# Finishing stages of a graph attention network: pairs written out in groups three ahead, own row scaled on ACT, no arithmetic on POOL, elu by a maximum

## The reference, cut to what matters

```
h = elu(layer_norm(x @ w_in + b_in, g_in, bt_in))
for i in range(3):
    identity = h
    hp = (h @ w_l[i]).reshape(N, 4, 64)
    s = sum(hp * a_s, -1); d = sum(hp * a_d, -1)
    e = leaky_relu(s[src] + d[dst], 0.2)
    alpha = softmax of e over the edges that enter a node, its own loop among them
    y = segment_sum(hp[src] * alpha[:, :, None], dst) + b_l[i]
    y = layer_norm(elu(y), g_l[i], bt_l[i])
    h = y + identity
```

## Time and profile before

| | us |
|---|---|
| median of 3 runs | 7346.19 (7344.77 to 7347.49) |
| profiled execution | 7350.6 |
| its span | 7348.8 |
| busy: PE, DVE, ACT, POOL | 5337.8, 4937.3, 4115.6, 3961.0 |
| input stage, first transfer to the next stage's first | 135.43 to 340.66 |
| finishing stage 0 | 1488.11 to 1720.37 |
| finishing stage 1 | 2883.43 to 3116.30 |
| finishing stage 2 (no projection) | 4275.47 to 4459.39 |

### The profile page before, as it was taken

How to read it: one execution, slowest core, us unless ns; L and a number is a source line. 1 busy time by engine, 2 the same in 40 slices (tenths; PEclk the granted TensorE clock), 3 DMA queues, 4 the chain that set the end, 5 groups by cost and what they waited for, 6 DMA issues and landing times. The chain is left out here.

```text
span 7348.8 us, 96874 instructions
## 1 busy us (share of the span) xinstructions
PE 5337.8 (73%) x22394; PEld 3800.7 (52%) x22394; DVE 4937.3 (67%) x13271; ACT 4115.6 (56%) x13250; POOL 3961.0 (54%) x3916
## 2 busy tenths in 40 slices
PE   1768888644888886468887614999978778777578
PEld 1645555333555554445555314888864566555335
DVE  5656666685777777667777576666652677877673
ACT  4578888844898987468989742333336222111132
POOL 3477777656777774677777730000000577777322
PEclk8878888866999998679999767999999898878789
DMA  6344444335444443354444422000017534333302
GB/s 177 116 126 118 117 118 117 89 111 145 118 119 120 119 121 86 118 143 121 119 120 118 109 88 71 23 17 26 17 54 260 164 114 127 105 105 98 93 14 78
DMA packets 492147, 774.74 MB, mean 105 GB/s; under 512 B 86183, under 2 KB 367735, under 8 KB 491703
## 3 DMA queue, kind: packets, MB, share of 16 engines
q0 software_dynamic: 168240, 452.12, 22.8%
q1 hardware_dynamic: 323607, 319.65, 13.9%
HBM read 634.42 MB, written 146.27 MB: 106 GB/s over the span
## 5 line engine op out<-in xcount | busy, mean ns | idle before, releaser
L1699 POOL DMA_INDIRECT gm_got<-scratch_feat,keep_src_tab x2520 | 2535.7, 1006 | 785.3 <-issue 680.0
L1910 ACT ACTIVATE gm_got<-gm_got 128x64 f32<-128x64 f32 x10080 | 2453.6, 335 | 4.7 <-DVE gm_got L1833 4.7
L1958 PE MATMUL gm_bank<-gm_got,gm_onehot 128*128 128x264 f32 x5040 | 1814.7, 467 | 388.7 <-DVE gat_acc L1856 230.1
L1958 PEld LDWEIGHTS gm_bank<-gm_got,gm_onehot 128*128 128x128 f32 x5040 | 950.8, 217 | 919.7 <-DVE gat_acc L1856 366.6
L1856 DVE TENSOR_TENSOR gat_acc<-gat_acc,gm_bank 128x264 f32 x2520 | 1072.1, 425 | 514.3 <-PE gm_bank L1958 238.8
L1032 POOL DMA_INDIRECT mix1a_got<-scratch_rel_feat,layer_rel_tab x240 | 238.2, 993 | 1392.5 <-issue 1391.0
L1032 POOL DMA_INDIRECT mix1b_got<-scratch_rel_feat,layer_rel_tab x600 | 616.3, 1027 | 193.6 <-issue 189.3
L1082 PE MATMUL mix1b_m_bank<-mix1b_got,mix1b_onehot 128*128 128x256 f32 x1200 | 394.2, 465 | 167.4 <-DVE layer_acc L1059 130.5
L1863 DVE TENSOR_TENSOR gm_onehot<-keep_iota_row,keep_dst_tab 128x896 f32<-128x896 f32 x360 | 389.4, 1082 | 28.3 <-PE gm_bank L1958 24.1
L1082 PEld LDWEIGHTS mix1b_m_bank<-mix1b_got,mix1b_onehot 128*128 128x128 f32 x1200 | 250.5, 227 | 277.0 <-DVE mix1b_onehot L1039 173.7
L3061 ACT ACTIVATE moe_h<-moe_first,moe_shift,moe_gain 128x512 f32<-128x512 f32 (+1 forms) x208 | 147.1, 758 | 344.2 <-PE moe_first L3103 344.2
(11 more groups left out here) (563 smaller groups left out, 11060.6 us busy)
## 6 DMA issues: line engine op xcount, KB each, us to landing
scratch_rel_feat<-rel_out SPq DMA_DIRECT2D x50, 1024.0 KB, 5.9
gm_got<-scratch_feat,keep_src_tab POOLq DMA_INDIRECT x2520
gm_flags<-scratch_flags SPq DMA_DIRECT2D x90, 280.0 KB
gf_feat<-scratch_feat SPq DMA_DIRECT2D x75, 256.0 KB, 4.2
gf_old<-scratch_hidden SPq DMA_DIRECT2D x75, 256.0 KB, 4.7
scratch_hidden<-gf_h SPq DMA_DIRECT2D x75, 256.0 KB, 3.9
scratch_feat<-gf_row SPq DMA_DIRECT2D x50, 260.0 KB, 3.7
gm_x<-scratch_x SPq DMA_DIRECT2D x50, 256.0 KB
```

The lines of the kernel that those rows point to most:

```text
L1699: nc.gpsimd.indirect_dma_start(out=got[:, place // GROUPS, place % GROUPS * GROUP + j, 0:GAT_ROW], out_offset=None, in_=dram["feat"][layer ...
L1910: last = nc.scalar.activation(rows, rows, ACT.Copy, scale=got[:, b, i, D + h:D + h + 1])
L1958: nc.tensor.matmul(bank[i % BANKS][:, 0:GAT_SUM], onehot[:, i % HOTS, :], got[:, v[1] % B, i, :], start=True, stop=True).then_inc(s_sum, 1)
```

## The change

It rewrites `gat_finish` and, in the same manner, the order in `gnn_input`; `Ring` and `Normalise` get counterparts `PairRing` and `GroupNorm` that count pairs.

- No hardware loops: each queue is written out for 25 pairs in six groups of 5, 5, 5, 5, 3 and 2.
- POOL only issues the scatters, straight from `scores` and `first_pos`, without copies and without waiting for earlier scatters. SP waits for sends and scatters only at the end of the stage.
- The own row is scaled on ACT, three groups ahead, 8 activations of 128x64 per pair. The bias becomes a pass of its own on DVE (128x512 per pair).
- elu is max(exp(-relu(-y)) - 1, y): ACT's relu of y is gone.
- `feat`, `old` and `y` hold ten pairs instead of five; feat is loaded four groups ahead, old three.
- One root and one reciprocal per group instead of per pair.
- In both stages the weights are loaded after the first five pairs of data, and DVE prepares the score weights later.

```diff
+PAIR_GROUPS = (5, 5, 5, 5, 3, 2)
+def flow(part, body):
+    for k in range(-4, len(PAIR_GROUPS)):
+        for name, ahead in body:
+            if 0 <= k + ahead < len(PAIR_GROUPS):
+                part(name, k + ahead)
...
 class Elu:
-        nc.scalar.activation(self.pos[:, u], y, ACT.Relu)
-        nc.scalar.activation(self.neg[:, u], y, ACT.Relu, scale=-1.0).then_inc(self.s_neg, 1)
+        nc.scalar.activation(self.neg[:, p % UNROLL], y, ACT.Relu, scale=-1.0).then_inc(self.s_neg, 1)
...
-        return nc.vector.scalar_tensor_tensor(out, self.neg[:, u], -1.0, self.pos[:, u], ALU.add, ALU.add)
+        return nc.vector.scalar_tensor_tensor(out, self.neg[:, p % UNROLL], -1.0, y, ALU.add, ALU.max)
...
 def gnn_input(nc, io, dram, keep, gathers, scores):
+                flow(part, [("load", 3), ("weights", 3), ("store", 0), ("send", 0)])
...
 def gat_finish(nc, io, dram, keep, gathers, layer, scores, acc, last_layer):
-    FIRST, LAST = ["sums", "norm"], ["turn", "project", "scores"]
-    BODY = [("turn", 0), ("sums", 1), ("project", 0), ("norm", 1), ("scores", 0)]
+    DVE_BODY = [("moments", 1), ("sums", 2), ("finish", 1), ("scores", 0), ("total", 2)]
+    ACT_BODY = [("root", 1), ("turn", 0), ("elu", 2), ("row", 0), ("scale", 3)]
+    DEEP = 2 * UNROLL
...
-                body = [("store", 0), ("feat", 2), ("stored", 0), ("send", 0), ("old", 2), ("sent", 0)]
+                flow(part, [("store", 0), ("feat", 4), ("weights", 4), ("old", 3), ("send", 0)])
...
             @block.gpsimd
-                                last = nc.gpsimd.tensor_tensor(one_tile(feat[:, u, i]), one_tile(feat[:, u, i]), spread(of_self, tile_at(r, u, i)), ALU.mult)
-                            nc.gpsimd.tensor_tensor(feat[:, u], feat[:, u], both(rows["b_l"][:, :]), ALU.add).then_inc(s_sum, 1)
+                    flow(lambda name, g: project.scatter_pool(pool, g), [("scores", 0)])
...
             @block.vector
+                            nc.vector.tensor_tensor(yp, yp, both(rows["b_l"][:, :]), ALU.add).then_inc(s_yb, 1)
...
             @block.scalar
+                        if name == "scale":
+                            act.wait_ge(s_feat[p % DEEP], landed(p))
+                            for i in range(PAIR):
+                                for k in range(H):
+                                    one = feat[:, p % DEEP, i, k * GAT_DIM:(k + 1) * GAT_DIM]
+                                    last = nc.scalar.activation(one, one, ACT.Copy, scale=of_self[:, p * PAIR + i, k:k + 1])
+                            last.then_inc(s_scaled, 1)
```

More of the change, by code:

```diff
@@ new lines, in scores_dve @@
+    def scores_dve(self, dve, g):
+        pairs = pairs_of(g)
+        u0, size = pairs[0] % UNROLL, len(pairs)
+        dve.wait_ge(self.s_mm, pairs[-1] + 1)
+        for p in pairs:
+            if p >= UNROLL:
+                dve.wait_ge(self.s_sent[p % UNROLL], reuse(p))
+        per = PAIR * 2 * GAT_HEADS
+        sc = self.score_bank[:, u0 * per:(u0 + size) * per].rearrange("p (t s) -> p t s", s=2 * GAT_HEADS)
+        self.nc.vector.tensor_copy(self.row[:, u0:u0 + size, :, D:].rearrange("p u i h -> p (u i) h"), sc[:, :, 0:GAT_HEADS])
+        self.nc.vector.tensor_copy(self.scores[:, pairs[0] * PAIR:(pairs[-1] + 1) * PAIR, :], sc).then_inc(self.s_sc, size)
@@ L2133, in _ @@
-                rounds(dve, part, FIRST, BODY, LAST)
+                        elif name == "total":
+                            elu.total(nc, p, yp, yp).then_inc(s_elu, 1)
+                        elif name == "moments":
+                            dve.wait_ge(s_elu, p + 1)
+                            ln.statistics(nc, p, yp)
+                        elif name == "finish":
+                            ln.finish(nc, p, yp, rows["bt_l"]).then_inc(s_ya, 1)
+                    for p in pairs_of(g):
+                        u, yp = p % UNROLL, y[:, p % DEEP]
+                        if name == "sums":
+                            dve.wait_ge(s_y, p + 1)
+                            dve.wait_ge(s_scaled, p + 1)
+                            nc.vector.tensor_tensor(yp, yp, feat[:, p % DEEP], ALU.add).then_inc(s_yf, 1)
+                        elif name == "moments":
+                            ln.aggregate(nc, p)
+                        elif name == "finish":
+                            dve.wait_ge(s_ya, p + 1)
+                            dve.wait_ge(s_old[p % DEEP], landed(p))
+                            if p >= UNROLL:
+                                dve.wait_ge(s_sent[u], reuse(p))
+                                if project:
+                                    dve.wait_ge(project.s_ht, p + 1 - UNROLL)
+                            nc.vector.tensor_tensor(h[:, u], old[:, p % DEEP], yp, ALU.add).then_inc(s_h, 1)
```

580 lines of the change are left out of this document (289 added, 291 removed).

## The result

The changed kernel takes **7226.8 us** (median of four runs, 7218.4 to 7229.4) against 7346.8 for the kernel before: ratio 0.9835, 95% interval 0.9818 to 0.9852, 120 us less or 1.65%. Forecast were 7195, a range of 7175 to 7245, and faster by more than 0.2% with a chance of 0.95. The sign and the range held; of the 151 us forecast, 31 did not come.

The account below looks back on a forecast made before the run. DVE was taken as the fullest engine, slowed beside POOL's arithmetic and otherwise waiting. Savings of 51 + 51 + 29 + 17 = 148, taken as 151 with overlaps, gave 7350.6 - 151 - 4.4 = 7195 us, range 7175 to 7245.

Parts of the forecast that it names:

- DVE's terms: Finishing stages: DVE's passes sum to 28.4 us per group of five pairs, including 3.08 for the added bias pass.
- POOL's arithmetic as the cause of the slow passes: Finishing stages: DVE runs slowly beside POOL's arithmetic, not transfers; ten multiplications take 9.31 us beside it, 3.43 without.
- ACT's durations: Finishing stages: 40 scalings at 0.24 us make 9.6 per group, table loads cost no drain, ACT's group is 23.1.
- ACT's order: Finishing stages: ACT's 23.1 us per group stay hidden under DVE's 28.4, since own rows are scaled a group ahead.
- the prediction's rival: ACT becomes the bound at 26.9 us per group, 29.5 with drains; about 10 a stage, 7225 in all; chance 0.10.
- There PE becomes the limit: Late groups of finishing 0 and 1: PE needs 2.7 us per pair, giving group 3's scores at 151.
- the last two pairs' scatters are not late: End of finishing 0 and 1: PE needs some 19 us for the last five pairs, POOL's 20 scatters 24.4.
- Input stage: Input stage: 17 us less, from 5 at PE's first projection, 7.7 scatters, 1.2 copies and 3 of PE's last run.
- Straight-line code itself I cost at nothing: Touched stages: writing out loops costs nothing; statistics of ten tiles take 3.35 us in straight-line code and in a loop.
- DVE did not stay slow: Rival: traffic, not POOL's arithmetic, slows DVE's passes, by 17 us a group, giving 7452; chance 0.03.
- Groups did not wait on one another: Rival: a ring or buffer reused too late keeps rounds at 34 us, giving about 7300; chance 0.03.
- Late loads or scatters: Rival: landings grow from 4 to 12 us or scatters take 1.5, costing 5 to 8 per stage, 7215; chance 0.06.

## Why the prediction was right, and where it fell short

**DVE's terms: right.** A group was put at 28.4, less 0.5 for overlaps, and took 27.73; the added bias pass took 3.08 (nearest row 3.08), ten multiplications 3.42. POOL's arithmetic as the cause of the slow passes was tested by itself and stands. Finishing 2 came at 152.3 (154.8 before overlaps), for which DVE alone was counted.

**ACT's durations: right; ACT's order: not followed through.** 40 scalings took 9.65 (forecast 9.6), a table load 1.28 with nothing paid beside it, as the trace of before had said against the drain that the Trainium skill, "ScalarE: Activation LUTs", section on what ACT_TABLE_LOAD costs, adds. (With these drains the prediction's rival has 26.9 + 2.8 = 29.7 a group, not 29.5.) ACT was never fuller than DVE: 118.60 against 146.93 in finishing 0. But I asked only whether DVE waits for ACT. The new 9.6 us stand ahead of the transposes' copies, for which TensorE waits.

**The step that failed in finishing 0 and 1** is "There PE becomes the limit: projecting a pair takes 1.81 to the scores and 0.95 for them, 2.7 in all". Those are rows at the upper clock, of the last pair of a round whose transposes came right before. In the new order TensorE idles first and begins at 1.2 GHz: 17.5 for five pairs and not 13.5. Scores of group 3 came at 157.4 and not 151, because the run began at 139.9 and not 137.4 and took 4 longer. Then "the last two pairs' scatters are not late" failed too: the copy of these scores precedes DVE's total of the next group, so POOL waited 3.9 for group 4's, and one scatter took 2.09. The last began 188.2 after the stage's start instead of 175.4: 6.4 by the late scores, 1.1 from them to the first scatter, 3.6 by POOL's wait beyond its usual gap and 1.7 by longer scatters. These 12.8 are the whole shortfall of 12.9 in finishing 0.

**Input stage: right in kind, 12.3 for 17.** The 5 at TensorE's first products of the input came: they begin 15.7 after the first transfer and not 20.6. But the sum took them for the whole stage, and at the first transposes of h (55.4 against 57.5) 2.0 were left. The 2.7 of the score weights, which were only to come later, stand on DVE between the two statistics of the first group: there the lead falls from 4.1 to 1.5. TensorE's shorter last run gave 2.3 for 3, the scatters' tail 8.0 for 8.9.

**"Straight-line code itself I cost at nothing": right on DVE, wrong for the kernel.** Where it stands it costs nothing. But it is code ahead of a later loop, whose place it shifted, and that cost 19.2 in a stage I had not looked at.

**What I had not forecast in its favour:** message stages 1 and 2, 9.8 and 9.9 shorter. In every version of the changed kernel outside the second chip they took 1153 to 1158 and 1147 to 1153, with the kernel before, moved loop or not, 1163 and 1158 to 1159. So it goes with the change. It is not instruction transfers, which are as many on that queue in both kernels (6 and 8); POOL is busy 7.2 and 8.8 us less there for the same 840 gathers. Why they are shorter no experiment asked, and it stays open. By the same token part of the agreement of the total is luck: 19.7 unforeseen one way and 19.2 the other.

**The rivals.** ACT did not become the bound, and DVE did not stay slow. Groups did not wait on one another as that rival had it, at 7300, but in the last groups DVE did wait for TensorE's scores, four times and 29.2 us in all; the order of DVE and ACT alone, which I had looked at, doesn't show that. "Late loads or scatters" was half right: scatters did stretch, to a mean of 1.44 us from 1.08, but mostly beside DVE's passes, where POOL has time; in the tail that I priced it was 1.7.

## What to carry to other kernels

When work is moved to an engine that has room, follow everything that queues behind it there, for every engine that waits, and not only the one that the change is meant to help. Price TensorE's work by rows at the clock that it will have: after waits of 4.1 to 10.9 us the next eight products took 3.1 to 3.8 us, mostly 3.75, in every run that kept the changed kernel's order, and not 1.97, and filling or closing the gap was worth 7 to 12 us in a stage of 190 to 196. The same code varied by 5.6 us from stage to stage, in step with how long its products ran slowly, so look for that before reading a small difference. And compare the stages that were not touched: a shift of 59 instructions in TensorE's stream (modulo 256) decided 19 us, and 27 useless transposes won them back.

## What the runs showed of the hardware

**A loop's place in the instruction stream.** The stage of the same loop of 1733 instructions took 1025 to 1027 us from places 211, 217 and 222 modulo 256, and 1044 to 1052 from 162 and 163, with 10 against 54 or 55 instruction transfers; the other places were not tried.

**Scatters stretch beside some DVE passes.** In the changed kernel's finishing 0 a scatter of 0.98 took 11.44, from 1560.86 to 1572.30; DVE's multiplications, additions and biases ran from 1561.99 to 1571.44. Two others, 3.89 and 2.96 long, end 0.9 after the residual and the total. Beside the statistics, the centring and the scaling they take 0.98 to 1.29. The Trainium skill, "SBUF — State Buffer", section on who interferes with whom, infers that DVE's tensor_tensor takes only the read side of the port that it shares with POOL, so that POOL can still write its descriptors. These rows speak against it: L2158, L2173, L2188 and L2183 are such passes. This is read from when they begin and end; no run took the passes away, and which property makes a pass hold a scatter up was not tried.

**The reverse.** POOL's arithmetic made DVE's centring of two SBUF tensors more than twice as long, 9.00 for 4.01, and ten multiplications 8.54 for 3.43.
